# A transformer layer on one core: the rows behind the last scores in another order and in freed score banks

## The reference

```python
out = jnp.einsum('bhij,bhjd->bhid', attn, v)
...
return out @ Wo.T + bo
...
def fp4_linear(x, w):
    xq = fp4_quant_dequant(x)
    wq = fp4_quant_dequant(w)
    return jnp.einsum('bsk,nk->bsn', xq, wq)
gate = fp4_linear(x, w_gate)
y = fp4_linear(x, w_up)
h = jax.nn.silu(gate) * y
return fp4_linear(h, w_down)
...
x = _layernorm(x + _L0_attn_ref(x, L0_attn_Wg, L0_attn_bg, L0_attn_Wv, L0_attn_bv, L0_attn_Wo, L0_attn_bo), axis=-1)
x = _layernorm(x + _L0_ffn_ref(x, L0_ffn_w_gate, L0_ffn_w_up, L0_ffn_w_down), axis=-1)
```

## Time and profile before

| | |
|---|---|
| runs | 391.77 us median of 3, 390.9 to 393.08 |
| the profiled execution | 388.9 us, its span 387.2 us |
| instructions | 8903 |
| TensorE busy | 329.0 us (85%) |
| VectorE busy | 285.7 us (74%) |
| ScalarE busy | 224.0 us (58%) |
| GpSimd busy | 188.0 us (49%) |
| granted TensorE clock, mean | 0.933 |
| last scores end, last output of ScalarE ends | 330 us, 382.8 us of the span |

### The profile page before, as it was taken

One profiled execution on the slowest core, in us unless ns is written; L12 is line 12 of the kernel. 1 busy time (PEld: TensorE's weight loads), 2 busy tenths in 40 slices (PEclk: granted clock), 3 DMA queues, 4 the chain that ended last, 5 costly groups with the idle time before them and its releaser, 6 DMA issues.

```text
span 387.2 us, 8903 instructions
## 1 busy us (share of the span) xinstructions
PE 329.0 (85%) x2964; PEld 195.8 (51%) x2964; DVE 285.7 (74%) x820; ACT 224.0 (58%) x498; POOL 188.0 (49%) x466
## 2 busy tenths in 40 slices
PE   6368786998899999999999999999998999857551
PEld 4233352554465656565656565656564656535341
DVE  1525547567879797979797979797979798889451
ACT  2034663466576767676767676767675777422210
POOL 7754033507273737373737474747473343543331
PEclk9999997799999999999999999999999999985555
DMA  4001000001000101010101010101010010000000
GB/s 117 27 1 29 14 2 3 27 2 29 1 30 3 42 1 42 2 44 1 42 2 43 1 43 2 43 0 30 3 29 13 15 30 2 14 14 3 14 14 17
DMA packets 12404, 7.62 MB, mean 20 GB/s; under 512 B 1026, under 2 KB 12356, under 8 KB 12356
## 3 DMA queue, kind: packets, MB, share of 16 engines
q1 hardware_dynamic: 12356, 7.03, 6.4%
HBM read 4.93 MB, written 2.10 MB: 18 GB/s over the span
## 4 chain that ended last, share of the span: by engine, by line
PE 34%; DVE 25%; POOL 18%; issue 13%; ACT 8%; POOLq 0%; ACTq 0%; DVEq 0%
PE OT L717 6%; PE S L694 5%; PE WA L824 4%; POOL nt L449 4%; PE S L698 3%; ACT Pm L545 3%; POOL rn L456 3%; POOL nt L451 3%; PE WC L737 2%; PE WD L795 2%; POOL nt L454 2%; POOL rstd L482 2%; DVE h L1065 2%; DVE xn L1113 2%; DVE A L1212 2%
## 5 line engine op out<-in xcount | busy, mean ns | idle before, releaser
L545 ACT ACTIVATE Pm<-S 128x384 f32<-128x384 f32 x256 | 111.8, 491 | 64.8 <-PE S L698 64.8
L694 PE MATMUL S<-mask,ident 128*128 128x384 f16 x256 | 65.8, 340 | 10.1 <-ACT Pm L545 7.9
L473 POOL TENSOR_TENSOR hq<-hm,hs 128x352 f32<-128x352 f32 x32 | 25.2, 787 | 66.0 <-DVE hm L1083 65.7
L717 PE MATMUL OT<-Pm,gv 128*32 128x256 f32 (+1 forms) x1024 | 56.8, 341 | 0.0
L698 PE MATMUL S<-BT,AT 32*128 32x256 f16 (+1 forms) x512 | 44.1, 251 | 0.0
L717 PEld LDWEIGHTS OT<-Pm,gv 128*32 128x32 f32 x1024 | 27.2, 111 | 21.2 <-issue 5.5
L698 PEld LDWEIGHTS S<-BT,AT 32*128 32x128 f16 x512 | 14.4, 93 | 42.9 <-issue 42.9
L694 PEld LDWEIGHTS S<-mask,ident 128*128 128x128 f16 x256 | 19.0, 99 | 33.7 <-issue 14.8
L1059 DVE SCALAR_TENSOR_TENSOR hh<-th,WC 128x352 f32<-128x352 f32 x32 | 16.6, 519 | 23.4 <-ACT th L563 23.3
L737 PE MATMUL WC<-wguT,xaT 128*128 128x352 f32 x64 | 29.1, 538 | 4.2 <-DVE h L1065 2.3
L795 PE MATMUL WD<-wdT,hqT 128*128 128x128 f32 (+1 forms) x192 | 29.6, 311 | 1.7 <-ACT hqT L593 1.7
(11 more groups left out here) (146 smaller groups left out, 715.0 us busy)
## 6 DMA issues: line engine op xcount, KB each, us to landing
xT<-x_turned_dram SPq DMA_DIRECT2D x16, 128.0 KB, 2.4
x_res<-x_dram SPq DMA_DIRECT2D x16, 128.0 KB, 2.1
out_dram<-yo SPq DMA_DIRECT2D x16, 128.0 KB, 2.1
wf<-w_down_dram SPq DMA_DIRECT2D x1, 176.0 KB, 2.5
wgv<-wgv_dram SPq DMA_DIRECT2D x1, 128.0 KB
wf<-w_gate_dram SPq DMA_DIRECT2D x1, 128.0 KB, 2.3
wf<-w_up_dram SPq DMA_DIRECT2D x1, 128.0 KB, 2.2
woT<-wo_dram SPq DMA_DIRECT2D x1, 64.0 KB
```

The costliest lines, as they stand in the source:

```text
L473: pool.tensor_tensor(b3(hq[:, k, 0:I]), b3(hm[:, k]), bc(hs[:, k], QB), ALU.mult).then_inc(s_hq, 1)
L545: act.activation(Pm[:, group % PR, hd % 4, :], S[:, (H * x + hd) % 3, 0:SCW], ACT.Exp, scale=1.0 / ZS).then_inc(s_exp, 1)
L694: pe.matmul(S[:, bank, 0:SCW], ident16[:, :], mask16[:, :], start=True, stop=False)
L717: i = pe.matmul(OT[VP * g:VP * (g + 1), T - (q1 - q0):T], gv_flat[:, at:at + VP], Pm[:, (GROUPS * x + c) % PR, g, q0:q1], start=(kt == 0 a ...
```

## The change

Only steps 16 to 19 get another order; in steps up to 15 TensorE's code is the same but for one more wait in the middle of each down projection. The parts:

1. The second gate/up half of batches 13, 14 and 15 goes to score banks 0 and 1 (`gate_up_at`). It no longer waits for `up` of the first half.
2. From step 17 on the second group of hq transposes goes to score bank 2. The down projection starts on its first half when the first copy of hq^T is there, not when both are (`k + 1 if t > B else NT`; up to step 16 the second wait is for the same count as the first).
3. In step 16 VectorE makes the attention output of batch 15 ahead of `quant_x` of batch 14, ScalarE copies a^T alone, and TensorE runs the output projection (now a function, `project`) right behind it, ahead of the x transposes and gate/up of batch 14.
4. In step 16 VectorE does the first residual and statistics of batch 15 between the pieces of `round_h(13)`, and in step 17 `quant_x` of batch 15 and the second residual of batch 13 stand ahead of `gate` and `up` of batch 14 (half 1). GpSimd makes batch 15's first scale ahead of batch 12's second, and ScalarE applies it (`apply_1`) ahead of the tanh of batch 14's half 1.

The diff, cut to its core (what is left out is the code that moved into `project`, `residual_1` and `residual_2`, and conditions `t != B + 1` on the lines that moved):

```diff
--- before.py
+++ after.py
@@ -324,6 +324,20 @@
...
                     return
+        def gate_up_at(x, k):
+
+            if k == 1 and x >= B - 3:
+                return S[:, 0, 0:I], S[:, 1, 0:I]
+            return WC[:, 0:I], WD[:, 0:I]
+
+        def h_done(x):
+
+            return NT * x + (2 if x < B - 3 else 1)
+
+        def copied(t):
+
+            return t if t <= B else t + 1
+
         def twice(t):
...
@@ -487,7 +501,7 @@
...
                     newton(t + 2, (0, 1, 2) if t < 0 else (0,))
-                if live(t - 2):
+                if live(t - 2) and t != B + 1:
                     rstd(t - 2, mv1, ve1, rstd1, nm1, nb1, s_ln1, 5 * (t - 2) + 5, s_rs1)
...
@@ -510,6 +524,8 @@
...
                     h_times_scale(t - 3, 0)
+                if t == B:
+                    rstd(B - 1, mv1, ve1, rstd1, nm1, nb1, s_ln1, 5 * B, s_rs1)
                 if live(t - 4):
...
@@ -557,15 +573,23 @@
...
                 act.activation(OTs[:, half, :], OT[:, 0:T], ACT.Copy).then_inc(s_ot, 1)
+            def apply_1(t):
+                act.wait_ge(s_rs1, 4 * (t - 2) + 4)
+                need(act, s_ln2, 5 * (t - 2 - YR) + 1)
+                need(act, s_xq, 9 * (t - 2 - YR) + 5)
+                ln_apply(y, rstd1, nb1, y1[:, (t - 2) % YR], s_y1)
+
             def tanh(x, k):
...
                 need(act, s_hh, NT * x + k - 1)
-                act.activation(th[:, k, :], WC[:, 0:I], ACT.Tanh, scale=0.5).then_inc(s_th, 1)
+                act.activation(th[:, k, :], gate_up_at(x, k)[0], ACT.Tanh, scale=0.5).then_inc(s_th, 1)
             for t in range(FIRST, LAST + 1):
...
                     exps(t, 0)
+                if t == B + 1:
+                    apply_1(t)
                 if live(t - 3):
...
@@ -579,15 +603,12 @@
...
                 exps(t, 2)
-                if live(t - 2):
-                    act.wait_ge(s_rs1, 4 * (t - 2) + 4)
-                    need(act, s_ln2, 5 * (t - 2 - YR) + 1)
-                    need(act, s_xq, 9 * (t - 2 - YR) + 5)
-                    ln_apply(y, rstd1, nb1, y1[:, (t - 2) % YR], s_y1)
+                if live(t - 2) and t != B + 1:
+                    apply_1(t)
                 exps(t, 3)
                 if live(t - 4):
-                    for k, bank in enumerate((WC, WD)):
+                    for k, bank in enumerate((WC, WD if t <= B else S[:, 2])):
                         act.wait_ge(s_hqT, NT * (t - 4) + k + 1)
...
@@ -598,7 +619,14 @@
...
                 exps(t, 5)
-                if live(t - 1) or live(t - 2):
+                if t == B:
+                    act.wait_ge(s_aT, t)
+                    need(act, s_wo, t - 1)
+                    act.activation(xaT[:, 0:T], WC[:, 0:T], ACT.Copy).then_inc(s_xac, 1)
+                    act.wait_ge(s_xqT, t - 1)
+                    need(act, s_gu, NT * (t - 2))
+                    act.activation(xaT[:, T:2 * T], WC[:, T:2 * T], ACT.Copy).then_inc(s_xac, 1)
+                elif live(t - 1) or live(t - 2):
                     c0, c1 = 0 if live(t - 1) else T, 2 * T if live(t - 2) else T
...
@@ -732,10 +760,22 @@
...
                 i.then_inc(s_ob, 1)
-            def gate_up(x, k):
+            def project(t):
+
+                after_last(pe, (t + 2, s_fit, 8 * (t + 2) + 1), (t + 1, s_BT, t + 2),
+                           (t - 2, s_ln1, 5 * (t - 2) + 1))
+                pe.wait_ge(s_xac, t)
+                for k in range(NT):
+                    pe.matmul(WB[:, k * D:(k + 1) * D], xaT[:, k * P:(k + 1) * P], woT[:, :],
+                              start=(k == 0), stop=False)
+                pe.matmul(WB[:, 0:T].rearrange("p (n d) -> p n d", n=NT), ones16[:, :],
+                          bias16[:, D:2 * D].rearrange("p (a d) -> p a d", a=1).to_broadcast([P, NT, D]),
+                          start=False, stop=True).then_inc(s_wo, 1)
+
+            def gate_up(x, k, g, u):
                 lhs = xaT[:, T + k * P:T + (k + 1) * P]
-                pe.matmul(WC[:, 0:I], lhs, wguT[:, 0:I], start=True, stop=True)
-                pe.matmul(WD[:, 0:I], lhs, wguT[:, I:2 * I], start=True, stop=True).then_inc(s_gu, 1)
+                pe.matmul(g, lhs, wguT[:, 0:I], start=True, stop=True)
+                pe.matmul(u, lhs, wguT[:, I:2 * I], start=True, stop=True).then_inc(s_gu, 1)
             def turn16(src, s_done):
@@ -749,8 +789,13 @@
...
                 if live(t - 3):
-                    pe.wait_ge(s_h, NT * (t - 3) + 1)
-                    gate_up(t - 3, 1)
+                    if t < B:
+                        pe.wait_ge(s_h, NT * (t - 3) + 1)
+                    else:
+                        pe.wait_ge(s_exp, H * B)
+                        if t > B:
+                            pe.wait_ge(s_h, NT * (t - 4) + 2)
+                    gate_up(t - 3, 1, *gate_up_at(t - 3, 1))
                 if t == 2:
...
@@ -767,8 +812,8 @@
...
                 if live(t - 4):
-                    after_last(pe, (t - 3, s_h, NT * (t - 3) + 2))
-                    for k, bank in enumerate((WC, WD)):
+                    after_last(pe, (t - 3, s_h, h_done(t - 3)))
+                    for k, bank in enumerate((WC, WD if t <= B else S[:, 2])):
                         pe.wait_ge(s_hq, NT * (t - 4) + k + 1)
...
@@ -789,8 +834,8 @@
...
                 if live(t - 4):
-                    pe.wait_ge(s_hqTc, NT * (t - 4) + NT)
                     for k in range(NT):
+                        pe.wait_ge(s_hqTc, NT * (t - 4) + (k + 1 if t > B else NT))
                         for n, (k0, kn) in enumerate(KC):
...
@@ -800,8 +845,8 @@
...
                     scores(0, 0)
-                wc_last = ((t - 4, s_hqTc, NT * (t - 4) + 1), (t - 3, s_h, NT * (t - 3) + 2),
-                           (t - 2, s_xac, t - 1))
+                wc_last = ((t - 4, s_hqTc, NT * (t - 4) + 1), (t - 3, s_h, h_done(t - 3)),
+                           (t - 2, s_xac, t - 1 + (t > B)))
                 if live(t - 1):
...
@@ -810,6 +855,8 @@
...
                     i.then_inc(s_aT, 1)
+                if t == B:
+                    project(t)
                 if live(t - 2):
...
@@ -854,9 +901,9 @@
...
                         pe.wait_ge(c_dve, 15)
-                    pe.wait_ge(s_xac, t)
-                    after_last(pe, (t - 4, s_ln2, 5 * (t - 4) + 1), (t - 3, s_h, NT * (t - 3) + 2))
-                    gate_up(t - 2, 0)
+                    pe.wait_ge(s_xac, copied(t) + (t == B))
+                    after_last(pe, (t - 4, s_ln2, 5 * (t - 4) + 1), (t - 3, s_h, h_done(t - 3)))
+                    gate_up(t - 2, 0, *gate_up_at(t - 2, 0))
                 scores(t, 7)
...
@@ -866,17 +913,8 @@
...
-                if live(t - 1):
...
+                if live(t - 1) and t < B:
+                    project(t)
                 values(t, 2)
@@ -1052,17 +1090,32 @@
...
-                dve.scalar_tensor_tensor(out=hh[:, :], in0=th[:, k, :], scalar=1.0, in1=WC[:, 0:I],
+                dve.scalar_tensor_tensor(out=hh[:, :], in0=th[:, k, :], scalar=1.0, in1=gate_up_at(x, k)[0],
-                dve.tensor_tensor(h[:, k, :], hh[:, :], WD[:, 0:I], ALU.mult).then_inc(s_h, 1)
+                dve.tensor_tensor(h[:, k, :], hh[:, :], gate_up_at(x, k)[1], ALU.mult).then_inc(s_h, 1)
@@ -1128,25 +1181,20 @@
...
+                if live(t - 2) and t != B + 1:
+                    residual_1(t - 2)
...
@@ -1163,6 +1211,13 @@
...
                     gate_up_weights()
+                if t == B + 1:
+                    for step in range(9):
+                        quant_x(t - 2, step)
+                    residual_2(t)
+                    ln_sums(t - 4, s_ln2, y2, st2)
+                    ln_aggr(t - 4, s_ln2, st2, mv2)
+
                 if live(t - 3):
...
@@ -1188,29 +1243,36 @@
...
+                if t == B:
+                    dve.wait_ge(s_ob, t)
+                    o = WA[:, 0:NT * H * OW].rearrange("p (q e) -> p q e", e=OW)
+                    dve.reciprocal(orec[:, :], o[:, :, HD]).then_inc(s_on, 1)
+                    dve.wait_ge(s_on, t)
+                    need(dve, s_aT, t - 1)
+                    dve.tensor_tensor(attn[:, :, :], o[:, :, 0:HD], bc(orec[:, :], HD), ALU.mult).then_inc(s_attn, 1)
+                if live(t - 2) and t != B + 1:
                     quant_x(t - 2, 0)
...
@@ -1221,19 +1283,20 @@
...
                     round_h(t - 3, 0, 2)
-                if live(t - 4):
-
-                    dve.wait_ge(s_dn, t - 3)
-                    need(dve, s_yo, NT * (t - 4))
-                    dve.tensor_tensor(y2[:, :, :], y1[:, (t - 4) % YR],
-                                      WD[:, 0:T].rearrange("p (n d) -> p n d", n=NT), ALU.add).then_inc(s_ln2, 1)
+                if live(t - 4) and t != B + 1:
+                    residual_2(t)
                 if live(t - 3):
                     round_h(t - 3, 0, 3)
-                if live(t - 4):
+                if live(t - 4) and t != B + 1:
                     ln_sums(t - 4, s_ln2, y2, st2)
+                if t == B:
+                    residual_1(B - 1)
```

(5 more changed lines are left out.)

41 lines of the change are left out of this document (18 added, 23 removed).

## The result

The change is faster: 388.49 us median of 15 runs (386.4 to 396.01) against 390.9 us for the kernel before (388.58 to 393.08, 15 runs), ratio 0.9928, 95% interval 0.99 to 0.9956. By the ratio that is 2.8 us (1.7 to 3.9); the two medians lie 2.4 us apart. The slowest execution of the change (396.01 us, a slower state that turns up now and then) is in the median and not in the ratio. 0.9 us of the distance is the base: three runs had shown 391.77 us as the median before.

A forecast was written before the change was run, and what follows sets the result against it. The prediction took VectorE to bound the tail. Its terms, +1.1 - 1.0 - 0.6 + 0.2, summed to -0.3 us (no change); 391.77 - 0.2 gave 391.6 us, range 389.3 to 393.1, chance of no change 0.73.

The forecast's parts named there:

- The clock: Around 346 us: where TensorE's upper clock is not granted, only the kernel before gets longer; -0.6 us, bounds 0 and -1.3.
- h(15): Tail up to batch 15's h complete: about 1.1 us later, between +0.2 and +2.0.
- The four waits: VectorE's tail waits in the new order: 2.6, 0.3, 1.2 and 0.8 us, 4.9 against 4.47 before, +0.4.
- lost overlaps: VectorE in the tail: grouping dependent work takes away about five overlaps of neighbouring instructions, +0.5 us.
- masks beside GpSimd: Rounding's exponent masks on VectorE in the tail, longer beside GpSimd's tensor work: +0.6 and -0.4, together +0.2 us.
- The chain behind h(15): From batch 15's h complete to the last output: -1.0 us, bounds -0.4 and -1.3.
- the wait at the second residual: Batch 14's second residual: its 0.41 us wait goes because the transposes no longer wait for `up(15, 1)`, -0.4 us.
- the split down projection: Batch 15's down projection starts at the first copy of hq^T instead of after the second: -0.55 us.
- The added wait: Inside each of 13 down projections up to step 16, always met: +0.2 us in all, bounds 0 and 3.3.
- rival B: Steady passes: the added wait breaks TensorE's stream, 0.25 us each, +3.3 us in all, 394.6 us; chance 0.08.
- The other parts: Batch 13's gate/up, earlier hq(12) transposes, a^T copied alone and early projection: at nothing, or 0.2 us; added wait +0.2.
- Rival A: Tail: the tanh waits go and only hn's replaces them, first wait below 0.9 us; 388.2 us, chance 0.15.

The follow-up runs named there:

- e13: Kernel before with extra unread matmuls in TensorE's tail waits, placed ahead of the wait for h: 385.47 us, ratio 0.9886, tail 47.96 us.
- e14: The change with extra unread matmuls in TensorE's tail waits, placed ahead of the wait for h: 387.21 us, ratio 0.9917, tail 49.28 us.
- e1: Kernel before run again with nothing edited, for a second profiled execution: 390.95 us, ratio 0.9994, tail 53.08 us.
- e3: Kernel before with only hq^T's second half in score bank 2 and the split down projection: 388.43 us, ratio 0.9949, tail 51.63 us.
- e15: Kernel before with only 22 unread matmuls added in TensorE's waits of the first 25 us: 385.15 us, ratio 0.9896, tail 53.10 us.
- e2: Kernel before with only the second gate/up half of batches 13 to 15 in score banks: 385.21 us, ratio 0.9872, tail 48.22 us.
- e4: Kernel before with gates in score banks, hq^T's score bank and the split down projection, nothing else: 385.06 us, ratio 0.9843, tail 47.77 us.
- e6: The change without the added wait in the down projection up to step 16: 387.15 us, ratio 0.9931, tail 50.96 us.
- e5: The change without batch 15's layer norm and x rounding ahead of batch 14's gates, and without the added wait: 383.91 us, ratio 0.984, tail 47.42 us.
- e7: The change without the added wait and with ScalarE's tail work in another order: 385.84 us, ratio 0.9872, tail 47.92 us.
- e8: e4 with 133 unread matmuls added in TensorE's tail waits: 382.87 us, ratio 0.9807, tail 45.07 us.

## Why the prediction was wrong

**The clock: the step that failed.** The term that was sized furthest off is that of the clock. "In executions where this stretch is not granted, before is up to 1.3 us longer and after is not" was the right mechanism, and e13 and e14 show it. It was priced at -0.6 us, half of the 1.27 us between the two lengths of batch 14's second half, since one execution could not tell how often the clock is granted. The three other profiled executions with this order of the gates and nothing filled in the tail (e1, e3, e15) all wait 2.10 us at batch 14's gate, 1.27 us more than the first, and e1's h(15) comes 1.21 us later. So the term was worth 1.2 us against them and not 0.6. That the upper level is the rarer case rests on these four executions alone. There was a sign that I passed over: the execution that the forecast was made from lay 2.9 us below the median of the runs, and I carried the difference over as a constant instead of asking which stretch it came from. e1, 2.2 us longer than that execution, shows that it came from two: 1.30 us before the tail and 1.21 us in it (0.3 comes back behind the last output).

The whole times can't say how often the stretch is granted. The 80 executions of the kernel before beside the experiments lie largely in two groups 2 us apart (33 from 388.2 to 389.2 us, 28 from 390.3 to 391.3). But the executions of the change do too (six from 386.4 to 387.2 us, six from 388.5 to 389.1), and the timelines show a step of that size in the head: of the 15 profiled executions without a filled head, five have the first residual of batch 0 at 66.80 to 67.52 us and ten at 69.04 to 70.35. e3 is one of the five, and its gate waits 2.10 us.

**h(15).** Forecast +1.1 us against the profiled execution, measured +0.56 (33.87 to 34.43). The four waits came out as priced: 2.6, 0.3, 1.2, 0.8 forecast, 2.62, 0.30, 1.22, 0.71 measured. The waits' +0.38 (4.85 against 4.47) leaves 0.18 for lost overlaps and for masks beside GpSimd, where I had put 0.7. The lower bound was added up wrong: waits of 4.2 us, no lost overlap and 0.2 for the masks make -0.1 and not +0.2. The masks of the earlier trace rows moved as said: batch 14's first is at 0.91 us (358.96).

**The chain behind h(15).** Forecast -1.0 us, measured -1.43 (18.00 to 16.57), beyond its bound of -1.3. e2 and e4 split it: the wait at the second residual 0.50 (18.00 to 17.50; I had 0.4), the split down projection 0.94 (17.50 in e2 to 16.56 in e4; I had 0.55). e3 reaches all 1.44 by the split alone, so the reason I gave for the first of these, that the transposes no longer wait for `up(15, 1)`, is enough but not needed. VectorE's wait for that matmul fell from 5.65 us (e1) to 4.71 (e3). Counted from the start of the transposes for the second copy, the timelines place it:

```profile
374.59 0.90 PE L774 MATMUL WD<-identf,hq 128*128 128x128 f32 x3 [1.97 <-POOL hq L473]
```
```profile
375.67 0.90 PE L819 MATMUL S<-identf,hq 128*128 128x128 f32 x3 [1.97 <-POOL hq L487]
```

Before, the twelve matmuls started 1.48 us after that (376.07) and took 2.93 us; now they start 0.70 us after it (376.37) and take 2.78. That is 0.78 and 0.15 us. I had let them start when these transposes end; by the timeline they start 0.20 us before that (375.67 + 0.90 = 376.57).

**The added wait and rival B.** +0.2 us was taken; e6 shows nothing, and the steady steps with the wait are the shortest of the four compared. Rival B, which wanted 3.3 us, is refuted.

**The other parts.** "At nothing" for a^T and the early projection: up to h(15) e5 (30.85 us) and e2 (30.72) show no gain. The wait of 1.19 us at batch 13's second gate was left out of the list of VectorE's waits; it did not change. TensorE's granted clock was read from the earlier trace rows as at its upper level until the last four slices: there are also two of 0.7 at 58 to 77 us, the fifth slice from the end is 0.8, and in the head the column does not show what the durations do (last section).

**Rival A** named the right size, 388.2 us, by luck (its four terms add up to 388.0), with the wrong mechanism: it wanted a first wait under 0.9 us, and that wait is 2.62. e7 shows what A needed: another order on ScalarE.

**The sum, mended.** +0.56 - 1.43 is the -0.87 us of the two profiled tails; with the clock at full price (1.21 us, by e1) it is -2.08 us, inside the measured 1.7 to 3.9. The forecast's sum was -0.3 (and -0.2 was carried into 391.6). Of the 1.78 us between, 0.61 is the clock, 0.54 h(15), 0.43 the chain behind it and 0.20 the added wait: the clock is the largest miss, but all four leaned the same way. The mechanisms of the first three were as forecast; a cost of the added wait did not show. The other 0.7 us to the 2.8 is not settled: the start of the tail varies by more than that from one execution to the next.

**What I did not ask** was what the change would be without its last part. The mechanism was read right and its worth was not: the banks give 4.86 us, the split another 0.94 behind h(15) (e2 to e4), and the reordering takes 3.2 (e4) to 3.6 (e5) back, because it sends the layer norm of batch 15 through two queues in which other work stands first. Part of what the banks give is again the clock: with TensorE's waits filled in both, the two parts together take 2.89 us off the tail (47.96 in e13 to 45.07 in e8), and 5.31 without (e1 to e4, where e4's slow stretch has already cost some 0.5).
